# First attention scores: the order of the prologue's projections, a chain of its own for 256 keys, and shorter row statistics

## The reference, cut to what matters

```python
xn = layernorm(x)                                   # (x - mean) / sqrt(var + 1e-5)
q, k, v = xn @ Wq.T, xn @ Wk.T, xn @ Wv.T           # 16 heads of 8 columns
q, k = rope(q), rope(k)                             # interleaved pairs: y*cos + swap(y)*sin
attn = softmax(q @ k.T / sqrt(8)) @ v
moe  = sum over the best two of 8 experts of gate * mlp_e(xn)   # three layers with gelu
out  = x + attn + moe
```

## Time and profile before

| | us |
|---|---|
| median of 3 runs | 632.62 (631.79 to 632.85) |
| span of the profiled execution | 630.1 |
| time outside the span (median less span) | 2.5 |
| PE, ACT, DVE, POOL busy | 597.7, 536.9, 338.4, 195.7 |

### The profile page before, as it was taken

The page is one execution under the profiler, slowest core; times in us unless marked ns, Lnnn a source line. Parts: engine busy times, 40 slices in busy tenths (PEclk is TensorE's granted clock), DMA queues, the critical chain, the costliest instruction groups (busy, mean ns, idle before and its releaser), DMA issues.

```text
span 630.1 us, 12248 instructions
## 1 busy us (share of the span) xinstructions
PE 597.7 (95%) x4152; PEld 259.9 (41%) x4152; DVE 338.4 (54%) x819; ACT 536.9 (85%) x548; POOL 195.7 (31%) x187
## 2 busy tenths in 40 slices
PE   9889999999999999998999999999999999999996
PEld 6323333232322222222799999993222222222221
DVE  5654233785343335121555555555494958668475
ACT  3799999999999999999554555559999999999995
POOL 2700000000554444441121222223645648484000
PEclk9999999999999999999999999999999999999999
DMA  8653711523363446693433333310312122121311
GB/s 230 172 196 136 264 36 35 217 101 119 127 218 124 146 147 211 211 302 67 105 81 71 79 75 75 75 44 22 104 36 87 48 69 63 58 84 57 113 44 35
DMA packets 82621, 70.67 MB, mean 112 GB/s; under 512 B 44288, under 2 KB 58400, under 8 KB 82576
## 3 DMA queue, kind: packets, MB, share of 16 engines
q1 hardware_dynamic: 76000, 56.34, 29.5%
q0 software_dynamic: 5856, 13.05, 6.8%
q10 hardware_dynamic: 720, 0.71, 0.5%
HBM read 32.92 MB, written 32.96 MB: 105 GB/s over the span
## 4 chain that ended last, share of the span: by engine, by line
PE 64%; ACT 16%; issue 10%; DVE 5%; DMA 2%; ACTq 0%; SPq 0%; DVEq 0%
PE ps L1496 13%; PE ps L1430 10%; ACT probs L731 9%; PE ps L1480 8%; PE ps L1553 6%; PE ps L1422 5%; PE ps L1443 5%; ACT probs L696 4%; PE ps L1526 4%; PE ps L1403 4%; PE ps L1347 2%; ACT probs L674 2%; DMA k_st<-k_d 2%; PE ps L1383 2%; PE ps L1310 1%
## 5 line engine op out<-in xcount | busy, mean ns | idle before, releaser
L696 ACT ACTIVATE probs<-ps 128x1536 f32<-128x1536 f32 (+1 forms) x154 | 206.1, 1426 | 6.7 <-PE ps L1480 6.3
L731 ACT ACTIVATE probs<-ps 128x1536 f32<-128x1536 f32 x140 | 190.2, 1520 | 2.0 <-PE ps L1526 1.9
L574 POOL DMA_INDIRECT slots_x_d<-xn_all,slot_i x64 | 62.5, 977 | 195.7 <-DVE expert_i L1037 127.2
L1496 PE MATMUL ps<-probs,v_st 128*32 128x512 f32 x896 | 119.5, 604 | 1.3 <-DVE v_st L839 0.7
L710 ACT ACTIVATE work<-ps,work 128x256 f32<-128x256 f32 (+1 forms) x156 | 64.9, 454 | 60.5 <-PE ps L1430 60.2
L1553 PE MATMUL ps<-probs,v_st 128*32 128x512 f32 x840 | 111.5, 604 | 0.5 <-DVE o_sb L922 0.5
L612 POOL DMA_INDIRECT work<-slots_y_d,slot_i x64 | 89.8, 1404 | 64.6 <-PE ps L1553 48.4
L1480 PE MATMUL ps<-q_st,k_st 32*128 32x512 f32 x448 | 77.2, 494 | 6.8 <-ACT probs L696 3.7
L1526 PE MATMUL ps<-q_st,k_st 32*128 32x512 f32 x420 | 71.1, 494 | 8.8 <-ACT probs L731 8.7
L1480 PEld LDWEIGHTS ps<-q_st,k_st 32*128 32x128 f32 x448 | 28.9, 181 | 114.6 <-ACT probs L696 80.0
L1526 PEld LDWEIGHTS ps<-q_st,k_st 32*128 32x128 f32 x420 | 26.4, 181 | 108.0 <-ACT probs L731 99.0
(11 more groups left out here) (193 smaller groups left out, 564.3 us busy)
## 6 DMA issues: line engine op xcount, KB each, us to landing
k_d<-parts SPq DMA_DIRECT2D x8, 1024.0 KB, 5.3
q_d<-parts SPq DMA_DIRECT2D x8, 1024.0 KB, 6.1
q_st<-q_d SPq DMA_DIRECT2D x30, 256.0 KB, 3.3
k_st<-k_d SPq DMA_DIRECT2D x30, 256.0 KB, 3.2
slots_x_d<-parts SPq DMA_DIRECT2D x5, 1024.0 KB, 7.5
work<-slots_x_d SPq DMA_DIRECT2D x128, 32.0 KB, 1.9
slots_y_d<-work POOLq DMA_DIRECT2D x32, 128.0 KB, 2.2
work<-work SPq DMA_DIRECT2D x24, 128.0 KB, 2.1
```

Of the source, the lines that this page charges most:

```text
L696: nc.scalar.activation(group_probs(phase, g)[:, 0:size, :], group_slot(g)[:, 0:size * HALF].rearrange("p (h n) -> p h n", n=HALF), ACT.Exp ...
L731: nc.scalar.activation(late_probs(g), group_slot(g).rearrange("p (h n) -> p h n", n=HALF), ACT.Exp, scale=SCALE).then_inc(S["exp_done"], 1)
L1496: ins = nc.tensor.matmul(o_ps[32 * h:32 * h + 32, :], v_window(mt, h, half), group_probs(phase, half * HALF_GROUPS + g)[:, n, :], start=(j ...
```

## The change

Row statistics: the additions of EPS and the halvings are folded into other operations; `std[:, 3]` holds 1/std, and the normalisation subtracts the mean and multiplies. Projections: PE projects the first queries (g = 1), then keys 0 to 255, keys 256 to 511, the values, and then g = 2 and g = 3. Keys 0 to 255 get their own signals (`k00_...`) through rotation, split and load; the rest of the first half follows. The load of the first queries moves from ACT's queue to the head of SP's. `WARM_AGAIN` falls from 4 to 2, with a wait for `proj_read` 2 ahead, and `scores(0, 0)` waits for `proj_read` 3, the next block for 4.

```diff
-WARM_AGAIN = 4
+WARM_AGAIN = 2
+START_KEYS = 2 * P
+        start_ps = [bank(2, 2), bank(0, 2)]
...
@@ SP
-            first_load(0, S["k00_loaded"], 0, P)
-            first_load(0, S["ka_loaded"], P, HALF)
+            first_load(1, S["q0_loaded"])
+            sp.wait_ge(S["k00_hi"], 1)
+            sp.wait_ge(S["k00_again"], 1)
+            sp.wait_ge(S["k00_lo"], 1)
+            sp.dma_start(k_st[:, 0:START_KEYS].bitcast(F32), parts[0:P // G, 0, :, 0:START_KEYS].bitcast(F32)).then_inc(S["k00_loaded"], 16)
+            first_load(0, S["ka_loaded"], START_KEYS, HALF)
             first_load(2, S["kb_loaded"])
@@ POOL
-            pool.wait_ge(S["proj_read"], 1)
-            rotate(0)
-            low_part(0)
+            pool.wait_ge(S["k00_read"], 1)
+            nc.gpsimd.tensor_tensor(rot[:, 0, 0:START_KEYS], t_cos[:, 0, 0:START_KEYS], t_sin[:, 0, 0:START_KEYS], ALU.add).then_inc(S["k00_rot"], 1)
+            pool.wait_ge(S["proj_read"], 2)
+            rotate(0, START_KEYS)
+            low_part(0, START_KEYS)
+            pool.wait_ge(S["k00_rot"], 1)
             square(0)
+            pool.wait_ge(S["k00_lo"], 1)
+            pool.wait_ge(S["k00_again"], 1)
             pool.wait_ge(S["proj_read"], 3)
             rotate(2)
@@ ACT
-            nc.scalar.activation(std[:, 0, 0:BT], std[:, 1, 0:BT], ACT.Sqrt).then_inc(S["std_made"], 1)
+            nc.scalar.activation(std[:, 0, 0:BT], std[:, 1, 0:BT], ACT.Sqrt, scale=0.25).then_inc(S["std_made"], 1)
...
-            high_part(0)
+            (the copies into b12 and head_r, moved here)
             high_part(1)
-            (the copies into b12 and head_r)
-            act.wait_ge(lo_made[1], 1)
-            act.dma_start(q_st[:, 0:HALF].bitcast(F32), parts[0:P // G, 1].bitcast(F32)).then_inc(S["q0_loaded"], 16)
+            act.wait_ge(S["k00_rot"], 1)
+            nc.scalar.activation(high(0)[:, 0:START_KEYS], rot[:, 0, 0:START_KEYS], ACT.Copy).then_inc(S["k00_hi"], 1)
+            nc.scalar.activation(high(0, 1)[:, 0:START_KEYS], rot[:, 0, 0:START_KEYS], ACT.Copy).then_inc(S["k00_again"], 1)
             for n in range(2):
                 act.wait_ge(S["v0_done"], n + 1)
...
+                if n == 0:
+                    high_part(0, START_KEYS)
             high_part(2)
@@ DVE, statistics
-                link(nc.vector.tensor_tensor(std[:, 0, t], stats[:, t, 1], stats[:, t, 4], ALU.add))
-                nc.vector.tensor_scalar(mean[:, t], std[:, 0, t], 0.5, None, ALU.mult)
-                link(nc.vector.tensor_tensor(std[:, 1, t], stats[:, t, 1], stats[:, t, 4], ALU.subtract))
-                link(nc.vector.scalar_tensor_tensor(std[:, 2, t], std[:, 1, t], 0.25, std[:, 1, t], ALU.mult, ALU.mult))
-                link(nc.vector.tensor_tensor(std[:, 3, t], stats[:, t, 2], stats[:, t, 5], ALU.add))
-                link(nc.vector.scalar_tensor_tensor(std[:, 0, t], std[:, 3, t], 1.0 / C, std[:, 2, t], ALU.mult, ALU.add))
-                nc.vector.tensor_scalar(std[:, 1, t], std[:, 0, t], EPS, None, ALU.add).then_inc(S["stats_made"], 1)
+                nc.vector.scalar_tensor_tensor(std[:, 3, t], stats[:, t, 2], EPS * C, stats[:, t, 5], ALU.add, ALU.add)
+                link(nc.vector.tensor_tensor(std[:, 0, t], stats[:, t, 1], stats[:, t, 4], ALU.subtract))
+                link(nc.vector.scalar_tensor_tensor(std[:, 2, t], std[:, 0, t], 0.25, std[:, 0, t], ALU.mult, ALU.mult))
+                nc.vector.scalar_tensor_tensor(std[:, 1, t], std[:, 3, t], 1.0 / C, std[:, 2, t], ALU.mult, ALU.add).then_inc(S["stats_made"], 1)
+                link(nc.vector.tensor_tensor(mean[:, t], stats[:, t, 1], stats[:, t, 4], ALU.add))
+                link(nc.vector.tensor_scalar(mean[:, t], mean[:, t], 0.5, None, ALU.mult))
@@ DVE, invert_first
-                link(nc.vector.tensor_tensor(std[:, 2, t], std[:, 3, t], std[:, 0, t], ALU.add))
-                link(nc.vector.tensor_scalar(std[:, 3, t], std[:, 2, t], 0.5, None, ALU.mult))
-                link(nc.vector.reciprocal(std[:, 2, t], std[:, 3, t]))
-                link(nc.vector.scalar_tensor_tensor(std[:, 3, t], mean[:, t], -1.0, std[:, 2, t], ALU.mult, ALU.mult))
+                link(nc.vector.scalar_tensor_tensor(std[:, 2, t], std[:, 3, t], 0.25, std[:, 0, t], ALU.mult, ALU.add))
+                link(nc.vector.reciprocal(std[:, 3, t], std[:, 2, t]))
@@ DVE, order
-            turn_parts(0)
-            turn_parts(1)
+            turn_parts(1, 1)
             rotate_first_queries()
-            turn_parts(2)
-            turn_parts(3)
+            turn_start_keys(0, 0)      # keys 0 to 255: cosines, then sines (signals k00_read)
+            turn_start_keys(0, 1)
+            low_first_queries()        # waits for hi_made[1]
+            turn_start_keys(1, 0)      # keys 256 to 511
+            low_start_keys()           # waits for k00_hi, signals k00_lo
+            turn_start_keys(1, 1)
+            turn_parts(2, 3)
+            turn_parts(3, 4)
@@ PE
-            for g in range(4):
-                first_projection(g)
+            first_projection(1, 1)
+            project_start_keys(0)
+            project_start_keys(1)
...
                 project_values(0, n, v0_ps[n]).then_inc(S["v0_done"], 1)
+            first_projection(2, 3)     # waits for k00_read
+            first_projection(3, 4)     # waits for proj_read 1
...
-                if (j == 0 and not (first and t == 0)) or (isinstance(t, int) and (t, j) == (0, 1)):
+                if (j == 0 and not (first and t == 0)) or (isinstance(t, int) and (t, j) == (0, 2)):
                     pe.wait_ge(S["ka_loaded"], t * 16 + 16)
...
+            pe.wait_ge(S["proj_read"], 2)
             for _ in range(WARM_AGAIN):
                 nc.tensor.matmul(bank(0), zeros[:, 0:P], xnT[:, 0, 0:HALF], start=True, stop=True)
+            pe.wait_ge(S["proj_read"], 3)
+            scores(0, 0, first=True)
             pe.wait_ge(S["proj_read"], 4)
-            scores(0, 0, first=True)
```

More of the change, by code:

```diff
@@ L331, in build @@
             rot_made0 rot_made1 hi_made0 hi_made1 again_made0 again_made1 lo_made0 lo_made1 sq_made0 sq_made1 parts_stored0 parts_stored1 parts_stored2 parts_stored3
-            exchanged0 exchanged1 parts_cleared k00_loaded v0_done v0_copied v0_read aux_done aux_read dve_chain dve_pro_chain
+            exchanged0 exchanged1 parts_cleared k00_loaded k00_proj k00_read k00_rot k00_hi k00_again k00_lo v0_done v0_copied v0_read aux_done aux_read dve_chain dve_pro_chain
             max_made exp_made masks_made routed zero_made x_zeroed x_scattered
@@ L527, in _, with rotate @@
             nc.gpsimd.memset(v_st[:, :, :, WIN + D:WIN + D + 1], 1.0).then_inc(S["st_init"], 1)
-            def rotate(g):
+            def rotate(g, lo=0):
                 u = g % 2
@@ L535, in rotate, with low_part @@
                     pool.wait_ge(sq_made[u], g // 2)
-                nc.gpsimd.tensor_tensor(rot[:, u, :], t_cos[:, u, :], t_sin[:, u, :], ALU.add).then_inc(rot_made[u], 1)
+                nc.gpsimd.tensor_tensor(rot[:, u, lo:HALF], t_cos[:, u, lo:HALF], t_sin[:, u, lo:HALF], ALU.add).then_inc(rot_made[u], 1)
                 pool.wait_ge(rot_made[u], g // 2 + 1)
-            def low_part(g):
+            def low_part(g, lo=0):
                 u = g % 2
                 pool.wait_ge(hi_made[u], g // 2 + 1)
-                nc.gpsimd.tensor_tensor(low(g), rot[:, u, :], high(g).bitcast(F32), ALU.subtract).then_inc(lo_made[u], 1)
+                nc.gpsimd.tensor_tensor(low(g)[:, lo:HALF], rot[:, u, lo:HALF], high(g)[:, lo:HALF].bitcast(F32), ALU.subtract).then_inc(lo_made[u], 1)
                 if g == 3:
@@ L802, in invert_rest @@
                     link(nc.vector.scalar_tensor_tensor(std[:, 2, t], std[:, 3, t], 1.5, std[:, 2, t], ALU.add, ALU.mult))
-                link(nc.vector.scalar_tensor_tensor(std[:, 3, t], mean[:, t], -1.0, std[:, 2, t], ALU.mult, ALU.mult))
+                link(nc.vector.tensor_copy(std[:, 3, t], std[:, 2, t]))
             def normalise_row_tile(k):
-                return nc.vector.tensor_scalar(xn_all[:, k, :], x_all[:, k, :], std[:, 2, k:k + 1], std[:, 3, k:k + 1], ALU.mult, ALU.add)
+                return nc.vector.tensor_scalar(xn_all[:, k, :], x_all[:, k, :], mean[:, k:k + 1], std[:, 3, k:k + 1], ALU.subtract, ALU.mult)
             statistics(0, BT)
@@ L1295, in weights, with first_projection @@
                 return wT[:, (2, 0)[g % 2] + swap, :]
-            def first_projection(g):
+            def first_projection(g, place):
                 u, m = g % 2, g // 2
                 pe.wait_ge(S["xnT0_made"], m + 1)
-                if g >= 2:
-                    pe.wait_ge(S["proj_read"], g - 1)
+                if g == 2:
+                    pe.wait_ge(S["k00_read"], 1)
+                elif g == 3:
+                    pe.wait_ge(S["proj_read"], 1)
                 for s in range(2):
@@ L1305, in first_projection, with project_start_keys @@
```

(7 more changed lines are left out.)

38 lines of the change are left out of this document (24 added, 14 removed).

## The result

The changed kernel's median is 633.95 us (631.51 to 637.53, 14 executions), against 632.62 (631.79 to 633.05, 14 executions): 1.0024 times as long, with an interval of 1.0013 to 1.0035. It is slower by about 1.3 us, where the prediction said 0.8 us faster. Measured a second time beside the kernel before, it was 1.0013 times as long, with an interval of 0.9996 to 1.0029 that includes no change; the second set alone doesn't tell the two apart. Each execution's time is 1.7 us (1.6 to 1.8) more than its span, so the profiled execution of before, with its span of 630.1, took about 631.8; that of after took 633.27.

A forecast was written before the change was run, and what follows sets the result against it. PE's queue was taken to set the first exponential, ACT the pace afterwards. The first exponential coming 0.77 us earlier made the span 630.1 - 0.77 = 629.3; with 2.5 outside, 631.85 us, range 630.4 to 633.1.

The forecast's parts named there:

- the line that sets the first exponential: Prologue, POOL then ACT: `high_part(2)` behind POOL's queue holds the first exponential until 23.70, 0.77 us earlier than 24.47.
- PE's queue: Prologue on PE: first scores reached at 21.96, 1.94 us earlier, so the exponential could start at 22.53.
- Rival 1: Prologue: PE's queue sets the start, POOL's half operations costing 0.52 each and turn-taking nothing; 630.8 us, chance 0.18.
- the turn between DVE and POOL: Prologue: DVE's rest of the queries and POOL's start-key sum don't run side by side; 0.4 us charged.
- statistics and loads: Normalised rows start about 0.97 us earlier, at 8.28; later loads keep slack of 1.2 us or more, costing nothing.
- rival 2: Step 0: gain given back by late second halves of queries or keys, or dearer POOL halves; 632.6 to 633.2, chance 0.16.
- It can't gain more: PE's start: the biases' load releases PE at 8.77, so PE gains 0.23 us at most from the shorter statistics.
- The prediction's 2.3: Prologue: PE stands 2.3 us between the first scores, done at 22.4, and the second, after 24.7; before, 1.3.
- rival 3: Step 0: PE's clock falls in the gap behind the first scores, halving speed for two blocks; 634.3 us, chance 0.09.
- 2.9 us: Delay from the end of PE's last work to the clock's fall, taken as the gap length that decides.
- two signs of being wrong: First exponential within 0.2 us of the end of its scores, or a later block waiting for a load.
- 2.5 us outside the span: Difference between the median of 632.62 and the span of 630.1, carried over unchanged into the forecast time.

The follow-up runs named there:

- e9_high2_pool_pad: Changed kernel with the two copies of `high_part(2)` made by POOL instead of ACT, and three small activations keeping ACT's program length: 631.27 us, 0.9966 of before.
- e3_fill_gap: Changed kernel with two multiplies of zeros added between PE's first and second scores: 632.81 us, 0.9993 of before.
- e4_warm0: Changed kernel with no multiplies of zeros ahead of the first scores instead of two: 634.56 us, 1.0020 of before.
- e8_fill_pad: e3_fill_gap with one more small activation early in ACT's program: 632.18 us, 0.9990 of before.
- e13_change_again: The changed kernel as it is, measured a second time beside the kernel before: 633.57 us, 1.0013 of before.
- e14_change_pad: Changed kernel with one more small activation on ACT, nothing else: 634.3 us, 1.0015 of before.
- e12_best: e9_high2_pool_pad with one multiply of zeros added between the first and second scores: 631.25 us, 0.9969 of before.
- e11_before_warm2_fill: Kernel before with two multiplies of zeros instead of four ahead of the first scores, and one between first and second scores: 631.56 us, 0.9978 of before.
- e6_before_stats: Kernel before with only the shorter row statistics of the change: 632.39 us, 0.9992 of before.
- e1_warm4: Changed kernel with four multiplies of zeros again instead of two: 633.14 us, 0.9999 of before.
- e2_before_warm2: Kernel before with two multiplies of zeros instead of four, nothing else: 632.61 us, 0.9986 of before.

## Why the prediction was wrong, by its own steps

**Right: the line that sets the first exponential.** The prediction had it held by `high_part(2)` behind POOL, at 23.70; it was, at 23.50 (how near that really is stands below). `e9_high2_pool_pad` takes that line away, and the start moves to 22.41, against the 22.53 that the prediction gave for PE's queue. POOL's queue in after:

```profile
15.50 0.73 POOL L560 TENSOR_TENSOR work<-work 128x256 f32<-128x256 f32 x1 [11.57 <-DVE work L838]
17.85 0.72 POOL L542 TENSOR_TENSOR work<-work 128x256 f32<-128x256 f32 x1 [1.63 <-DVE work L838]
19.18 0.73 POOL L549 TENSOR_TENSOR parts<-work,parts 128x256 fp32r<-128x256 f32 x1 [0.60 <-ACT parts L661]
19.87 1.03 POOL L557 TENSOR_TENSOR squares<-work 128x512 f32<-128x512 f32 x1
21.07 1.34 POOL L542 TENSOR_TENSOR work<-work 128x512 f32<-128x512 f32 x1 [0.17 <-POOL squares L557]
```

The half sums took 0.72 and 0.73 (0.68 estimated), `square(0)` 1.03 (1.04), `rotate(2)` 1.34 (1.26). All but `square(0)` took a little more than estimated. Rival 1 fell with that.

**Right: the turn between DVE and POOL.** DVE's rest of the queries began with POOL's 0.73:

```profile
15.51 1.26 DVE L851 TENSOR_TENSOR parts<-work,parts 128x512 fp32r<-128x512 f32 x1
```

It took 1.26 us where the same shape alone took 0.69: put off by 0.57 (0.4 charged). The prediction's sum had POOL second; here DVE was, and it had found both to give nearly the same. By the Trainium skill, "SBUF — State Buffer", section "Who interferes with whom", the order of issue decides who is blocked. The trace agrees, with POOL starting at 15.50 and DVE at 15.51.

**Right in effect: statistics and loads.** The normalisation began at 8.24 (8.28 predicted). The later loads had their slack: no wait in step 0, so rival 2 didn't occur in this kernel.

**A bound that wasn't one.** "It can't gain more" than 0.23, said the prediction of PE's start, because the biases' load releases PE at 8.77. In after it did so at 8.36. Over the traces the release lies between 8.35 and 9.73: one landing time was taken for a constant. It matters, because with the shorter statistics the whole line to the first exponential hangs on this load. In the six traces in which ACT's queue sets that start (after, `e3_fill_gap`, `e4_warm0`, `e8_fill_pad`, `e13_change_again`, `e14_change_pad`), it lies 15.13 to 15.15 us behind the release: 23.50 behind 8.36, 23.87 behind 8.73, 24.87 behind 9.73. So 0.41 of the 0.97 us by which after led comes from a load that landed earlier than in before (8.36 against 8.77). With the release at 8.73, about where the prediction had it, the first exponential came at 23.87 and the lead was 0.60: the forecast of 23.70 was 0.17 too early, and that after came out on its other side is luck.

The idle time on PE doesn't depend on the landing: it is 2.65 or 2.66 us in after, `e13_change_again` and `e14_change_pad`. The prediction's 2.3 was short because the exponential is later against the first scores. In `e13_change_again` these start at 21.86 (21.96 predicted), but the second scores come at 25.02, where 24.7 was predicted.

**The step that failed: rival 3.** Its mechanism is what happened; its condition and chance were wrong. The prediction saw the gap of over 2 us coming, and said that the clock "decides if the gap reaches" 2.9 us, read from the one place where PE had stopped for good. But with 2.66 us of idle time 31 of 38 executions fell (change 21 of 26, `e14_change_pad` 10 of 12), with the first exponential of their profiles at 23.50 to 23.89, before the 24.3 that the rival asked for. So the 2.9 us of that row weren't the point from which the clock decides, and the forecast's sum put the clock at nothing without a reason that holds. Over all runs the executions that fell are these (idle time on PE around the first scores, by the profiles; where two are given, ahead of the first and ahead of the second):

| idle time on PE | kernels | fell |
|---|---|---|
| 0.2 us | `e12_best` | 3 of 12 |
| 0.65 us | `e3_fill_gap`, `e8_fill_pad` | 5 of 24 |
| 0.85 and 0.23 us | `e11_before_warm2_fill` | 0 of 11 |
| 1.29 us | before, `e6_before_stats`, `e1_warm4`, `e9_high2_pool_pad` | 29 of 130 |
| 0.89 and 1.28 us | `e2_before_warm2` | 7 of 12 |
| 2.66 us | change, `e14_change_pad` | 31 of 38 |
| 1.77 and 2.52 us | `e4_warm0` | 12 of 12 |

With 1.29 us or less in all, 37 of 177 fell, about as many at 0.2 as at 1.29; with 2.17 us or more, 50 of 62. (`e12_best` has two waits of 0.5 us for loads later in step 0, and falls elsewhere count too, so the few falls of the upper rows needn't come from this gap.) Before, one execution in five already fell, which one profile with the clock at 1.00 can't show. By these counts rival 3 deserved far more than 0.09. Its price was too high: 2.6 us for two blocks at half clock, where the pair of profiles gives 1.17. Half speed for 3.4 us is 1.7 us of PE work; that the rest lay beside exponentials which ACT still had to do is an estimate, not a run. That the rival's 634.3 lies near the measured 633.95 is therefore in part luck: the late steps, which it didn't know of, make up for its price.

**Not foreseen: the late steps.** About 1 us was lost between 440 us and the end, 0.6 of it by ACT's program being one instruction shorter. No step of the prediction looked at ACT's instruction count; all of its reasoning ended at 40 us. So even where the clock held, the lead of 0.6 to 0.97 us was mostly gone at the end: the changed kernel's median span is 630.8 then (five executions), against 631.1.

**Its own signs.** The prediction named two signs of being wrong, a first exponential right behind its scores and a later block that waits for a load. Neither appeared, and what it said would show it right mostly did: the normalisation at 8.24, DVE's rest stretched, the gap of over 2 us at clock 1.00. Only the first row transpose came sooner, at 9.01 and not near 9.4. All these signs end with the gap; the clock fell behind it.

**The sum.** A little over half of the executions changed sides: 22% fell before, 81% after. By the mean spans of the held and the fallen, before makes 0.78 x 631.1 + 0.22 x 632.9 = 631.5, the change 0.19 x 630.5 + 0.81 x 632.8 = 632.4: 0.9 longer, against 0.8 (`e13_change_again`) and 1.5 (first run) by the ratios. The direction is accounted for; of the size of the first run some 0.6 us is not. The fallen are longer than the held by about 2 us, more than the 1.17 of the one fall that was isolated. In the first run nine of the 14 executions show a mean clock of 0.995 or less, below the 0.996 of the profiled one, so there may have been longer or further falls in them, as `e14_change_pad` shows one near 190 us; they weren't profiled.

The prediction's "2.5 us outside the span" was the distance of one short execution from the median: 1.7 lie outside, and the rest was that execution's own.

## What to carry to other kernels

A wait that is taken off one engine becomes idle time on another: work that only fills time (here two multiplies of zeros) can be what keeps TensorE's clock, so move it into the new gap instead of dropping it. Better still, take the work ahead of the first use off the queue that has become late, as `e9_high2_pool_pad` does, which halves the gap and had the largest gain on before. Where an event happens in some executions only, count executions by their clock before explaining a median, and compare the traces to their ends, not only around the edit. And before two traces are compared, look at what the whole line hangs on: here one small load's landing moves the first exponential by over a microsecond between executions of like kernels.

## What the runs showed of the hardware

- The granted clock fell after PE had resumed: idle from 21.99 to 24.65, at 1.00 until about 25.85, then 0.50 until about 29.26. Looking only at the idle stretch shows nothing.
- Whether it falls varies between executions of one program with the same idle time (2.65 and 2.66 us, held and fallen). What else decides it stays open; 3 of 12 executions of `e12_best` fell with 0.2 us of idle time at the first scores, and no run shows where in the span they did.
- ACT's idle time in a loop at 460 us depends on whether its program has 1175 or 1176 instructions: 0.62 and then 0.40 us a step against 0.32. What the stalled exponential waits for was done by then: its scores ended at 464.04 in after and it began at 464.47, where before these were 463.63 and 463.75. The instruction-fetch packets of the traces fall into the same two groups: one of 8 KB on queue q14 starts 0.76 to 1.01 us ahead of that exponential in the eight traces with 1176 instructions, and 0.62 to 0.65 us behind it in the five with 1175. That fetching across the loop is the cause fits this, but as the packet comes behind the idle time, no run shows it.
- The biases' load at the start of the program releases PE anywhere within 1.4 us (8.35 to 9.73), and in the changed prologue the first exponential follows it, 15.13 to 15.15 us behind in six traces.
